# Cross-attention kernel for ten selected rows per batch: the opening rebuilt with one-hot row picking, 64-column tiles and another transfer order

## The reference

```python
scores = jnp.einsum('bnd,d->bn', base_hidden, score_w[0]) + score_b[0]
_, topk_idx = jax.lax.top_k(scores, TOPK)                       # TOPK = 10
sparse_hidden = jnp.take_along_axis(base_hidden, topk_idx[:, :, None], axis=1)
q = sparse_hidden @ Wq.T + bq ; k = ctx @ Wk.T + bk ; v = ctx @ Wv.T + bv    # split into 16 heads
attn = softmax(q k^T / sqrt(32))
attn_out = (attn v) @ out_w.T + out_b
return base_hidden.at[batch, topk_idx].set(attn_out)
```

## Time and profile before

| what | value |
|---|---|
| time, median of 3 runs | 163.79 us (161.93 to 164.19) |
| the profiled execution's own time | 164.43 us |
| its span, first to last instruction | 162.2 us |
| PE busy | 151.5 us (93%), 1204 records |
| DVE busy | 83.6 us (52%) |
| ACT busy | 22.8 us (14%) |
| mean granted TensorE clock | 0.947 |
| moved by DMA | 37.05 MB, mean 228 GB/s |

### The profile page before, as it was taken

The page is one execution under the profiler, slowest core; times in us unless marked ns, Lnnn a source line. Parts: engine busy times, 40 slices in busy tenths (PEclk is TensorE's granted clock), DMA queues, the critical chain, the costliest instruction groups (busy, mean ns, idle before and its releaser), DMA issues.

```text
span 162.2 us, 2819 instructions
## 1 busy us (share of the span) xinstructions
PE 151.5 (93%) x1204; PEld 147.1 (91%) x1204; DVE 83.6 (52%) x215; ACT 22.8 (14%) x47; POOL 4.2 (3%) x13
## 2 busy tenths in 40 slices
PE   3679999899998999999999999999999989999990
PEld 3679999899998999999999999999999979998950
DVE  3481030099799924460679817805724740872440
ACT  3000003100021310320021300400400310131100
POOL 3002000000002000000000000000000000000002
PEclk9969985559999999999999999999999999999999
DMA  4997599999999998300499999999999989993001
GB/s 120 313 401 194 136 417 340 257 241 235 215 229 299 358 264 207 124 4 0 121 355 216 268 353 215 232 353 214 246 281 241 224 270 248 334 405 162 4 0 40
DMA packets 5487, 37.05 MB, mean 228 GB/s; under 512 B 850, under 2 KB 850, under 8 KB 2940
## 3 DMA queue, kind: packets, MB, share of 16 engines
q1 hardware_dynamic: 4936, 36.11, 76.7%
q10 hardware_dynamic: 380, 0.40, 1.2%
q0 software_dynamic: 160, 0.37, 0.8%
HBM read 33.04 MB, written 3.83 MB: 227 GB/s over the span
## 4 chain that ended last, share of the span: by engine, by line
PE 74%; DMA 16%; DVE 6%; issue 1%; POOLq 1%; SPq 0%; ACT 0%; DVEq 0%
PE logits_ps L589 26%; PE mix_ps L608 24%; DMA ctx_c<-ctx_cols_dram 13%; PE logits_ps L483 6%; DMA x_sb<-x_dram 4%; PE misc_ps L569 2%; PE logits_ps L635 2%; PE logits_ps L523 2%; PE misc_ps L523 2%; PE misc_ps L538 2%; PE mix_ps L538 2%; PE logits_ps L557 1%; PE mix_ps L557 1%; DVE product L295 1%; PE misc_ps L623 1%
## 5 line engine op out<-in xcount | busy, mean ns | idle before, releaser
L589 PE MATMUL logits_ps<-qk,ctx_c 128*125 128x160 f32 x384 | 55.8, 307 | 0.8 <-DMA ctx_c<-ctx_cols_dram 0.8
L589 PEld LDWEIGHTS logits_ps<-qk,ctx_c 128*125 128x125 f32 x384 | 54.9, 195 | 1.1 <-DMA ctx_c<-ctx_cols_dram 1.0
L608 PE MATMUL mix_ps<-probs,ctx_r 125*128 125x160 f32 x384 | 54.3, 300 | 0.0
L608 PEld LDWEIGHTS mix_ps<-probs,ctx_r 125*128 125x128 f32 x384 | 52.6, 190 | 0.6 <-issue 0.5
L370 DVE TENSOR_REDUCE col_max<-logits_ps 125x160 f32<-125x960 f32 x8 | 9.2, 1154 | 26.8 <-PE logits_ps L589 26.8
L409 DVE TENSOR_REDUCE prob_sum<-probs 125x160 f32<-125x960 f32 x8 | 14.5, 1830 | 4.0 <-ACT probs L260 4.0
L483 PE MATMUL logits_ps<-ones 128*128 128x128 f32 x90 | 14.3, 330 | 2.5 <-DVE row_base L438 2.5
L264 ACT ACTIVATE mix<-mix_ps 128x320 f32<-128x320 f32 x16 | 7.0, 438 | 65.1 <-PE mix_ps L608 65.1
L483 PEld LDWEIGHTS logits_ps<-ones 128*128 128x128 f32 x90 | 13.6, 242 | 2.5 <-POOL row_base_i L207 2.5
L260 ACT ACTIVATE probs<-probs 125x480 f32<-125x480 f32 x16 | 9.3, 603 | 36.5 <-DVE probs L403 36.5
L295 DVE CUSTOM_DVE_ANT_0 product<-x_sb,score_w_sb 112x512 f32<-112x512 f32 x16 | 10.0, 689 | 3.8 <-DMA score_w_sb<-score_w_dram 3.5
(11 more groups left out here) (79 smaller groups left out, 87.1 us busy)
## 6 DMA issues: line engine op xcount, KB each, us to landing
ctx_c<-ctx_cols_dram SPq DMA_DIRECT2D x8, 1500.0 KB, 14.2
ctx_r<-ctx_rows_dram SPq DMA_DIRECT2D x8, 1440.0 KB
x_sb<-x_dram SPq DMA_DIRECT2D x8, 448.0 KB, 12.1
out_dram<-x_sb SPq DMA_DIRECT2D x8, 448.0 KB, 13.9
wq_sb<-wq_dram SPq DMA_DIRECT2D x1, 1024.0 KB, 8.5
wk_sb<-wk_dram SPq DMA_DIRECT2D x1, 1024.0 KB, 10.9
wv_sb<-wv_dram SPq DMA_DIRECT2D x1, 1024.0 KB, 14.8
wo_sb<-wo_dram SPq DMA_DIRECT2D x1, 1024.0 KB, 16.5
```

The costliest lines, as they stand in the source:

```text
L589: last = nc.tensor.matmul(logits_ps[n][0:S_P, t // BANK_T, (t % BANK_T) * HQ:(t % BANK_T + 1) * HQ], ctx_c[n][:, f, t, :], qk[:, b, f, :], ...
L608: last = nc.tensor.matmul(mix_ps[half][:, f * HQ:(f + 1) * HQ], ctx_r[n][:, t, c:c + P], probs[n][:, t, :], start=(t == 0), stop=(t == S_T ...
```

## The change

Group 0 no longer gathers its rows from DRAM. The row numbers are spread over 112 partitions by a product (`spread_idx`), compared there with each row's own number (`mark_rows`, DVE), and the resulting one-hot matrices pick the rows out of `x_sb` (`pick_rows`: eight products of 32 one-hot columns by 256); ACT and DVE copy half each to `parts`, and `join_rows` (8 products of 64-column weights by 20) transposes and joins them. The projection of both groups and the fold of group 0 use weights 64 columns wide, two column tiles side by side. `spread_queries` is two wide operations per half, a bias addition and a product with `head_mask`. The fold of group 0 keeps four banks and is copied in four pieces instead of eight, and `first_logits` starts with the first piece. The key bias is kept transposed (32 partitions by head column), which changes `dot_key_bias`, `copy_key_dot` and `find_shift`. `score_w` is loaded as one row and spread by a product and an ACT copy; the score bias is added before the transposes; DVE waits for the biases' transfer before the first `score`. Warm-up products are 256 columns wide: 9, 5 and 1. Group 1's scores are transposed and its row numbers made inside weigh 1; its rows are transposed and projected after weigh 1. SP no longer waits for a gather; context rows go in four transfers per batch; wv, wo and five output copies are issued before context columns 4. Declarations, bank assignments and GpSimd's constants (`row_name_i`, `one_hot`, `regroup`, `head_mask`) are left out below.

```diff
-WARM_SCORES, WARM_CHOICE, WARM_GATHER = 11, 14, 18
+WARM_SCORES, WARM_CHOICE, WARM_N = 9, 5, 256
+FIRST = GROUPS[0][1]
+PART = 32
+TILE = 64
 CTX_MAIN = 120
+EARLY_COPIES = 5
...
-                sp.dma_start(ctx_r[n][0:CTX_MAIN, :, :], ctx_rows[b, 0:CTX_MAIN, :, :]).then_inc(ctx_r_in[n], 16)
-                sp.dma_start(ctx_r[n][CTX_MAIN:S_P, :, :], ctx_rows[b, CTX_MAIN:S_P, :, :]).then_inc(ctx_r_in[n], 16)
+                for part in (slice(0, CTX_MAIN), slice(CTX_MAIN, S_P)):
+                    for t in range(0, S_T, BANK_T):
+                        sp.dma_start(ctx_r[n][part, t:t + BANK_T, :], ctx_rows[b, part, t:t + BANK_T, :])\
+                            .then_inc(ctx_r_in[n], 16)
...
             sp.dma_start(wk_sb[:, :, :], wk).then_inc(wk_in, 16)
-            load_x(GROUPS[1][0], GROUPS[1][0] + 2)
-            sp.wait_ge(gathered[0], 16)
             load_cols(0, 0)
+            load_x(2, 6)
             load_cols(1, 1)
-            load_x(GROUPS[1][0] + 2, B)
             load_rows(0, 0)
+            load_x(6, B)
             load_rows(1, 1)
...
             sp.wait_ge(logits_done, 1)
             load_cols(2, 0)
-            for b in range(2, B):
-                if b + 1 < B:
-                    sp.wait_ge(logits_done, b)
-                    load_cols(b + 1, (b + 1) % 2)
-                sp.wait_ge(mix_ready[1], b - 1)
-                load_rows(b, b % 2)
-                copy_x(b - 2)
-            copy_x(B - 2)
-            copy_x(B - 1)
+            sp.wait_ge(logits_done, 2)
+            load_cols(3, 1)
+            sp.wait_ge(mix_ready[1], 1)
+            load_rows(2, 0)
+            sp.wait_ge(mix_ready[1], 2)
+            load_rows(3, 1)
             sp.dma_start(wv_sb[:, :, :], wv).then_inc(wv_in, 16)
             sp.dma_start(wo_sb[:, :, :], wo).then_inc(wo_in, 16)
+            for b in range(EARLY_COPIES):
+                copy_x(b)
+            sp.wait_ge(logits_done, 3)
+            load_cols(4, 0)
+            for b in range(5, B):
+                sp.wait_ge(logits_done, b - 1)
+                load_cols(b, b % 2)
+                sp.wait_ge(mix_ready[1], b - 2)
+                load_rows(b - 1, (b - 1) % 2)
+                copy_x(EARLY_COPIES + b - 5)
+            sp.wait_ge(mix_ready[1], B - 2)
+            load_rows(B - 1, (B - 1) % 2)
...
             exponential(0, 0)
             copy_mix(0, 0)
             exponential(1, 1)
...
+            copy_mix(1, 1)
             copy_queries(1)
-            copy_mix(1, 1)
...
+                dve.wait_ge(idx_spread, 1)
+                nc.vector.tensor_tensor(
+                    one_hot[:, :, :, 0:TOPK],
+                    idx_ps.rearrange("p (b q) -> p b q", b=FIRST).unsqueeze(2).broadcast_to([X_P, FIRST, 2, TOPK]),
+                    row_name[:, :, :].unsqueeze(3).broadcast_to([X_P, FIRST, 2, TOPK]), ALU.is_equal).then_inc(hot_done, 1)
...
+                    nc.vector.tensor_tensor(
+                        q_sb[g][:, es, :, :], query_ps[g][half][:, 0:2 * nb * TOPK].rearrange("p (t b q) -> p t b q", t=2, b=nb),
+                        bias_sb[:, 0, es].unsqueeze(2).unsqueeze(3).broadcast_to([P, 2, nb, TOPK]), ALU.add).then_inc(q_biased, 1)
+                    dve.wait_ge(q_biased, 2 * g + half + 1)
+                    nc.vector.tensor_tensor(
+                        q_diag[g][:, es, :, :, :].rearrange("p t b h q -> p (t b) h q"),
+                        q_sb[g][:, es, :, :].rearrange("p t b q -> p (t b) q").unsqueeze(2).broadcast_to([P, 2 * nb, HPT, TOPK]),
+                        head_mask[:, :].unsqueeze(1).unsqueeze(3).broadcast_to([P, 2 * nb, HPT, TOPK]), ALU.mult)\
+                        .then_inc(q_done, 1)
...
+                nc.vector.tensor_tensor(biased_max[:, :], all_max[:, :], key_dot[:, b, :], ALU.add).then_inc(max_step, 1)
+                dve.wait_ge(max_step, at + 7)
+                nc.vector.tensor_tensor(head_shift[0:QUAD, :], key_dot[:, b, :], biased_max[:, :], ALU.subtract)\
                     .then_inc(max_step, 1)
...
+            dve.wait_ge(bias_in, 16)
+            nc.vector.tensor_copy(key_rep[:, :, :], bias_sb[:, 1, :].unsqueeze(2).broadcast_to([P, DT, QUAD]))\
+                .then_inc(key_rep_done, 1)
+            dve.wait_ge(vec_consts, 4)
+            dve.wait_ge(score_w_done, 1)
+            dve.wait_ge(score_b_in, 16)
             score(0)
             score(1)
-            dve.wait_ge(score_b_in, 16)
             choose_eight(0)
             choose_rest(0)
-            move_idx(0)
-            dve.wait_ge(bias_in, 16)
-            nc.vector.tensor_copy(key_rep[:, :, :], bias_sb[:, 1, :].unsqueeze(2).broadcast_to([P, DT, S_P]))\
-                .then_inc(key_rep_done, 1)
+            mark_rows()
+            copy_parts()
+            dve.wait_ge(mask_done, 1 + HPT)
             spread_queries(0)
             copy_key_dot(0)
...
             find_max(0, 0)
             find_shift(0)
             subtract_max(0, 0)
+            score(6)
+            find_max(1, 1)
+            find_shift(1)
+            subtract_max(1, 1)
+            score(7)
             choose_eight(1)
             choose_rest(1)
-            find_max(1, 1)
-            move_idx(1)
-            find_shift(1)
-            subtract_max(1, 1)
+            move_idx()
...
+            def pick_rows():
+                pe.wait_ge(hot_done, 1)
+                for half in range(2):
+                    for b in range(FIRST):
+                        for j in range(2):
+                            at = (2 * b + j) * PART
+                            last = nc.tensor.matmul(parts_ps[half][at:at + PART, :], one_hot[:, b, j, :],
+                                                    x_sb[:, b, j, half * (D // 2):(half + 1) * (D // 2)],
+                                                    start=True, stop=True)
+                    last.then_inc(parts_ps_done, 1)
+
+            def join_rows():
+                pe.wait_ge(regroup_done, 2 * FIRST + 1)
+                pe.wait_ge(parts_done, 2)
+                for t in range(DT):
+                    for j in range(P // TILE):
+                        last = nc.tensor.matmul(picked_ps[0][j * TILE:(j + 1) * TILE, t * FIRST * TOPK:(t + 1) * FIRST * TOPK],
+                                                parts[:, t * P + j * TILE:t * P + (j + 1) * TILE],
+                                                regroup[:, :, :].rearrange("p b q -> p (b q)"), start=True, stop=True)
+                last.then_inc(picked_T_ps, 1)
+
...
+                            for j in range(P // TILE):
+                                c = e * P + j * TILE
+                                last = nc.tensor.matmul(query_ps[g][half][j * TILE:(j + 1) * TILE, k * nq:(k + 1) * nq],
+                                                        wq_sb[:, t, c:c + TILE], picked_T[g][:, t, b0 * TOPK:b1 * TOPK],
+                                                        start=(t == 0), stop=(t == DT - 1), skip_group_check=True)
...
+                    pe.wait_ge(q_done, half + 1)
+                    for step in range(QK_STEPS):
+                        for e in range(2 * half, 2 * half + 2):
+                            for j in range(P // TILE):
+                                c = step * P + j * TILE
+                                last = nc.tensor.matmul(fold_ps[step][j * TILE:(j + 1) * TILE, e * w:(e + 1) * w],
+                                                        wk_sb[:, e, c:c + TILE],
+                                                        q_diag[0][:, e, :, :, :].rearrange("p b h q -> p (b h q)"),
+                                                        start=True, stop=True)
+                        if half:
+                            last.then_inc(qk_ps, 1)
...
+            def first_logits():
+                pe.wait_ge(ctx_c_in[0], 16)
+                for f in range(DT):
+                    pe.wait_ge(qk_done, f + 1)
+                    for t in range(S_T):
...
-            keep_warm(WARM_GATHER)
-            transpose_picked(0)
-            keep_warm(2)
+            spread_idx()
+            pick_rows()
+            keep_warm(1)
+            join_rows()
             pe.wait_ge(wq_in, 16)
             project_queries(0)
             pe.wait_ge(wk_in, 16)
             fold_keys()
             dot_key_bias(0)
-            pe.wait_ge(qk_done, QK_UNITS)
-            logits(0, 0, {})
-            logits(1, 1, {2: lambda: transpose_scores(1)})
-            weigh(0, 0, {4: lambda: move_idx(1)})
-            weigh(1, 1, {12: lambda: transpose_picked(1), 18: lambda: project_queries(1)})
+            first_logits()
+            pe.wait_ge(key_rows_done, DT)
+            logits(1, 1, {})
+            weigh(0, 0, {})
+            weigh(1, 1, {1: lambda: transpose_scores(1), 12: move_idx})
+            transpose_picked()
+            project_queries(1)
             fold_pairs()
             dot_key_bias(1)
```

(4 more changed lines are left out.)

272 lines of the change are left out of this document (141 added, 131 removed).

## The result

| | before | after |
|---|---|---|
| median | 163.1 us (4 runs, 161.93 to 164.19; three of them gave the 163.79 above) | 166.83 us (4 runs, 164.86 to 168.37) |
| ratio after to before | | 1.020, interval 1.013 to 1.028 |
| profiled execution, its span | 164.43, 162.2 us | 166.73, 164.9 us |
| mean granted clock | 0.947 | 0.947 |
| logits 2 starts | 71.66 us | 75.22 us |

The forecast was 162.0, a small gain; its range ended at 167.0. The whole difference arises before logits 2: +3.56 us there, -0.8 for the context columns that no longer come late ahead of logits 7, which makes +2.76; the spans differ by 2.7.

The account below looks back on a forecast made before the run. PE was taken to bound the kernel, with the opening and group 1's stage deciding. Logits 2 earlier (-1.0) and no wait ahead of logits 7 (-0.8): 164.43 - 1.8 = 162.6, median 0.64 lower, 162.0 us; range 156.0 to 167.0.

Parts of the forecast that it names:

- Biases land at 9.5: Opening: the biases, which the first score waits for, land at 9.5 us (bounds 8 and 10.5), 1.0 us given back.
- Row numbers 15.3, `spread_idx` 16.0, projection 19.2: Group 0's opening: times in us of row numbers, their spreading and the projection's start (bounds 17.5 and 21; before 19.48).
- Projection and fold at half clock: Group 0: projection takes 3.4 us, ending 22.6, and fold 4.3 us, so logits 0 begins at 27.4 instead of 32.17.
- clock holds: Rival: PE keeps the full clock from 19.2 on, logits 2 starts at 64.9, time 156.2 us; chance 0.31, nearly so included.
- Weigh 1 at W = 48.3, rows 1 at 44.5: Weigh 1 starts at 48.3, 7.0 us early, behind weigh 0; by the transfer sum, context rows 1 landed by 44.5.
- such a wait as a sign of being wrong: Sign: the prediction is wrong if PE waits for a context transfer, rows 1 or columns 4.
- The gather, issued at W + 4.6, lands in 7.3: Group 1's gather: issued 4.6 us after weigh 1 starts, landed 7.3 us later, PE idle 4.5 us.
- The stage from landing to logits 2: 8.45 at the full clock, 2.0 for the clock: Group 1, transposes through key bias: 8.45 us plus 2.0 for half clock, logits 2 at 70.7 against 71.66.
- The 0.8 us ahead of logits 7 goes: Main part: PE's 0.8 us wait for context columns ahead of logits 7 disappears, as output copies no longer crowd there.
- Group 1's gather decides: Rival: half clock to the end of `fold_pairs`, slower logits 0, logits 2 at 77.0, time 168.3 us; chance 0.14.
- the turning point: Weigh 1's start to logits 2: the change loses where this stage exceeds 24.2 us, with weigh 1 at 48.3.
- Tiles don't overlap: Rival: projections stay at 3.5 us and the fold at 7.1, logits 2 at 75.1, time 166.4 us; chance 0.08.

Follow-up runs that it names:

- rows whole: The changed kernel with context rows in two transfers per batch, as before, instead of four: 171.82 us, ratio 1.055.
- spreading alone: The changed kernel with only wv, wo and five output copies moved behind context columns 4 and spread over the batches: 169.67 us, ratio 1.040.
- columns first: The version with early choice, late bias wait and spread transfers, with context columns 1 moved ahead of x 6 and x 7: 158.79 us.

## Why the prediction was wrong

The direction of nearly every part was right, and the sum came out on the wrong side. The working, term by term:

- *Biases land at 9.5.* 11.0: nothing was given back by the smaller `score_w`. The upper bound of 10.5 was too low by 0.5. No cost at the end (168.16 without the wait).
- *Row numbers 15.3, `spread_idx` 16.0, projection 19.2.* 17.2, 18.3 and 21.8: 1.5 us from the biases, and the warm-up products ran at half clock, 3.87 us for five, as the forecast had allowed. From `spread_idx` to the projection I had 3.2; it took 3.4.
- *Projection and fold at half clock.* They ran at the full clock: 2.05 us and some 2.4 instead of 3.4 and 4.3. Logits 0 at 26.3, not 27.4. This is the rival "clock holds", as far as it went; of seven profiled executions with this code up to logits 0, two (rows whole, spreading alone) stayed at half until 30.4 and 30.7.
- *Weigh 1 at W = 48.3, rows 1 at 44.5.* 48.1, but for another reason: PE was ready at 46.3 and waited for rows 1, which came 3.6 us after the forecast; I had named such a wait as a sign of being wrong. My sum of transfers left out what else was moving: SP had issued all of rows 1 by 18.0 and columns 2 at 42.1, the DMA share was 0.98 throughout, and by 48.1 it had moved 284 GB/s for 46.1 us, 13.1 MB, where my sum has 11.9. The 1.2 MB are 4.2 us at that rate, an estimate that would account for the 3.6; no run held columns 2 back. The number hit by luck, the step did not.
- *The gather, issued at W + 4.6, lands in 7.3.* Issued at W + 4.6 (52.7), landed in 9.8. **This is the first term that failed, +2.5 us.** I took the higher end of the earlier trace rows as the price on a full DMA. Seven more kernels with this gather uncovered and nothing held back gave 6.9 to 11.0, the one with rows 2 held back 3.2. The Trainium skill gives for a transfer's cost a fixed 2.0 us plus its bytes over 436 KB per us ("DMA: Bandwidth & Descriptors", the anatomy of one DMA); for 160 KB that is an estimate of 2.4 us. With rows 2 held back the same 160 KB took 3.2; on the full DMA it was four times the estimate. The 2.7 that I took as the price on a quiet DMA was that of group 0's gather, which has 20 rows where this one has 80.
- *The stage from landing to logits 2: 8.45 at the full clock, 2.0 for the clock.* It took 12.7. **The second term that failed, +2.3 us.** The mechanism (half clock behind a gap) was there; its size was not. The run with products of ones in the gap had 9.2 at the full clock, so my 8.45 was 0.8 short and half clock cost 3.5, not 2.0.
- *The 0.8 us ahead of logits 7 goes.* It went.

The two terms are 4.8 us, and the span after (164.9) is 4.5 above my forecast of it (162.2 - 1.8 = 160.4). The rest cancels.

Which rival came true? *Group 1's gather decides*, by the place of the loss: the stage from W to logits 2 took 27.1 us, over the 24.2 from which I had the change lose, and over the 25.4 that the rival itself allowed. Its sum didn't come true: it took all of the excess from the clock, none from the landing, and a W of 51.6 from a slow logits 0. Its 25.4 with the W of 48.1 would have given 164.8, so that its 168.3 lies near the measured 166.8 is in part luck. I gave it 0.14. What should have raised that: all the evidence for it stood in the trace before, where this gather was hidden, and the margin of my own forecast to the turning point (22.35 against 24.2) was less than the spread between the two landings that I had seen, 2.7 and 7.3. *Tiles don't overlap* is refuted: 32 ns a record in the projection against 110 in the earlier trace rows, and 7 to 9 us lost without them. The Trainium skill says that weight loads overlap running products only between different row groups ("TensorE: Matmul & The Clock Gate", Part 3); all the column tiles here share one row group, and the trace disagrees.

The order of what counts is shown by runs: the late selection alone costs 13.7 us in the kernel before; the tiles are worth 7 to 9 in the changed one; without the gather the change would be 2% faster than the kernel before; with the choice early, the transfers spread and the bias wait gone it is 1.8% faster. That the transfers bind the opening is borne out by two versions in which one wait of the opening went and another transfer's took its place (no bias wait: rows 1; columns first: x 6). Not settled: what decides whether the opening keeps the full clock, what made rows 1 late, and whether the half-length context rows help.

## What to carry to other kernels

A gather whose issue is moved behind the last work that covers it costs its landing on a full DMA (here 7 to 11 us, not the 3.2 with the other transfers held back), and then the half clock that the gap leaves in the thin products behind it; price both before trading it for a shorter opening. Where the transfers are busy from end to end, a gain in the arithmetic only stays if the transfer that comes next is early too: look for the landing that becomes the floor, and expect each removed wait to turn up at the next transfer. Weights 64 columns wide in two column tiles shorten thin products that loads bound (2.05 us instead of 3.52 here); the time shows it only where no transfer is next, and in the kernel before alone it showed nothing.

## What the runs showed of the hardware that I had not expected

- Two column tiles of 64 need 32 ns a record, 2.05 us for 64, where 128-column weights need 110 ns, 3.52 for 32: for the same work 1.7 times faster. At half clock, with 60 columns, 58 ns against 221 ns, nearly twice.
- The landing of 160 KB, gathered row by row, varied from 3.2 us with context rows 2 held back to 6.9 to 11.0 with the DMA full.
- The same opening ran at the full clock from 17.6 us in one execution, and at half from 13.8 to 30.7 in another. Its five warm-up products behind the transposes took 2.35 us in three kernels, 3.77 to 4.02 in three and 4.50 in two, and PE's idle time before them (2.9 to 4.3 us) doesn't sort them.
- With products of ones in the gap the clock was full at its end; it fell 4.3 us after the start of a thin stage of 128-column loads, and not in one of 64-column tiles (one execution each).
- Behind waits of 4.0 to 4.7 us for context rows 1, 22 records of weigh 1 took 4.58 to 5.41 us; behind one of 1.8 us they took 3.00, at the full clock.
